# Weight loads of a grouped feed-forward: casting loads on GpSimd's queue replaced by raw int32 loads on SyncE's and casts on VectorE and ScalarE

## What is computed

```python
xn = _layernorm(x, axis=-1)
s = _L0_attn_ref(xn, ...)          # 16 heads, causal
wg = w_gate.astype(f32) / 127      # (3072, 1024) int32, values -127..127
wu = w_up.astype(f32) / 127        # (3072, 1024) int32
wd = w_down.astype(f32) / 127      # (1024, 3072) int32
h  = silu(xn @ wg.T) * (xn @ wu.T)
g  = silu(h @ wd.T)
x  = x + s * g
```

## Time and profile before

| | us |
|---|---|
| median of two timed runs | 3277.18 (3241.79 and 3312.57) |
| profiled execution, whole | 3240.19 |
| its span, slowest core | 3238.7 (cores from 3217.6) |
| PE, DVE, ACT, POOL busy | 2219.3, 880.1, 928.4, 114.0 |

### The profile page before, as it was taken

The page is one execution under the profiler, slowest core; times in us unless marked ns, Lnnn a source line. Parts: engine busy times, 40 slices in busy tenths (PEclk is TensorE's granted clock), DMA queues, the critical chain, the costliest instruction groups (busy, mean ns, idle before and its releaser), DMA issues.

```text
span 3238.7 us, 38701 instructions; the slowest of 8 cores (3217.6 to 3238.7 us)
## 1 busy us (share of the span) xinstructions
PE 2219.3 (69%) x14643; PEld 1170.7 (36%) x14790; DVE 880.1 (27%) x1701; ACT 928.4 (29%) x1245; POOL 114.0 (4%) x216
## 2 busy tenths in 40 slices
PE   2499899984666546786777777065634565877777
PEld 0244444432233213464664665032322221333333
DVE  1544444442232264433222112500200000122122
ACT  2111111102111145463443444132232123222222
POOL 0000011100000000000000000000010000000000
PEclk9699999997878865656556555587856885888888
DMA  4222222202111020202001000533252102011010
GB/s 121 28 30 30 30 33 36 35 3 52 20 17 17 1 52 2 60 2 59 2 2 60 2 2 14 158 56 52 33 81 30 26 0 52 1 52 42 11 52 27
DMA packets 58440, 111.83 MB, mean 35 GB/s; under 512 B 7561, under 2 KB 15755, under 8 KB 55700
## 3 DMA queue, kind: packets, MB, share of 16 engines
q0 software_dynamic: 34112, 52.44, 11.5%
q1 hardware_dynamic: 24148, 56.90, 5.5%
HBM read 142.88 MB, written 18.88 MB: 50 GB/s over the span
## 4 chain that ended last, share of the span: by engine, by line
PE 55%; ACT 17%; DVE 13%; issue 8%; DMA 7%; DVEq 1%; ACTq 0%; SPq 0%; POOL 0%; PEldq 0%; POOLq 0%
PE PS L890 8%; PE PS L724 6%; ACT EB L912 6%; PE PS L1190 6%; PE PS L596 5%; PE PS L605 5%; PE PS L1333 4%; PE PS L1402 4%; PE PS L639 4%; PE PS L1273 2%; DMA PLAND<-Wsel 2%; ACT PRJ L732 2%; DVE PS L895 2%; DVE ACC L650 1%; PE PS L956 1%
## 5 line engine op out<-in xcount | busy, mean ns | idle before, releaser
L890 PE MATMUL PS<-Q,K 64*128 64x128 bf16 x2176 | 274.3, 305 | 125.1 <-ACT EB L912 120.1
L1190 PE MATMUL PS<-XN,W1FULL 128*128 128x512 bf16 x749 | 186.9, 409 | 158.3 <-DMA W1FULL<-Wk 80.1
L912 ACT ACTIVATE EB<-PS,negBh 128x1152 bf16<-128x1152 f32 (+7 forms) x128 | 204.0, 1594 | 258.1 <-DVE PS L895 242.6
L890 PEld LDWEIGHTS PS<-Q,K 64*128 64x128 bf16 x2176 | 211.8, 136 | 154.4 <-issue 143.7
L639 PE MATMUL PS<-HT,WDT 128*128 128x512 bf16 x745 | 191.0, 390 | 38.8 <-DVE HT L622 21.9
L724 PE MATMUL PS<-XN,WBLK 128*128 128x512 bf16 x746 | 207.8, 443 | 12.8 <-DVE K L739 5.1
L895 DVE TENSOR_TENSOR PS<-PS,trinegT 128x128 f32<-128x128 f32 x256 | 76.6, 300 | 439.7 <-PE PS L890 434.6
L596 PE MATMUL PS<-XN,WGT 128*128 128x512 bf16 x752 | 170.6, 382 | 8.5 <-DVE ACC L650 5.6
L1190 PEld LDWEIGHTS PS<-XN,W1FULL 128*128 128x128 bf16 x768 | 78.5, 104 | 263.8 <-issue 189.9
L605 PE MATMUL PS<-XN,WUT 128*128 128x512 bf16 x752 | 168.8, 379 | 0.8
L650 DVE TENSOR_TENSOR ACC<-ACC,PS 128x512 f32<-128x512 f32 x224 | 149.0, 686 | 35.7 <-PE PS L639 34.1
(11 more groups left out here) (162 smaller groups left out, 2579.6 us busy)
## 6 DMA issues: line engine op xcount, KB each, us to landing
PLAND<-Wsel POOLq DMA_DIRECT2D x64, 256.0 KB, 4.2
XF<-xT SPq DMA_DIRECT2D x1, 8192.0 KB, 33.0
XT<-xT SPq DMA_DIRECT2D x4, 2048.0 KB, 10.3
x1park<-XT SPq DMA_DIRECT2D x32, 256.0 KB
X1CH<-x1park SPq DMA_DIRECT2D x8, 1024.0 KB, 8.6
XT<-x1park SPq DMA_DIRECT2D x4, 2048.0 KB, 8.4
outT<-XT SPq DMA_DIRECT2D x32, 256.0 KB
LAND<-wg POOLq DMA_DIRECT2D x16, 256.0 KB, 5.8
```

The lines of the kernel that those rows point to most:

```text
L890: tS = P.op("tensor", lambda t, h=h, gi=gi, tt=tt, off=off: t.matmul(PS[:, off + tt * 128:off + (tt + 1) * 128], head_k(h, ts(tt, 128)), h ...
L912: s.activation(EB2[:, slot, 0:klen], PS[:, 0:klen], AF.Exp, bias=negBh[:, h:h + 1]), inc=True)
L1190: P.op("tensor", lambda t, fc=fc, j=j, n=n: t.matmul(BK(n), W1FULL[:, j, ts(fc, 128)], src_xn[:, j, ts(n, 512)], start=(j == 0), stop=(j = ...
```

## The change

A slice is now loaded by SP as raw int32 into ILAND, a new area of two slots in unused room of the V region. A cast on DVE or ACT, in turn (`cflip`), then writes it as bf16 into the landing buffer, and PE transposes from there as before. All these loads share one new semaphore, dw2. The cast of slice i waits for the whole count of dw2 so far issued, and for PE's reads of its landing buffer. The load of slice i+2 is placed on SP's queue after the cast of slice i, whose slot it reuses. `prep_issue2` issues two loads ahead of a gate/up stage. The first four slices of group 0 are still casting loads of POOL; two raw loads for slices 4 and 5 are issued once the layer norm has read the V region (`tk_var0`).

```diff
-                            lambda li, wsrc=wsrc, hc=hc: P.dma(
-                                "gpsimd", LANDX(li),
+                            lambda il, wsrc=wsrc, hc=hc: P.dma(
+                                "sync", ILAND[:, il, :],
                                 wsrc[hc * 128:(hc + 1) * 128, :],
-                                sem=f"dl{li}")))
+                                sem="dw2")))
...
+    def prep_issue2(g):
         sl = p2_slices(g)
+        P.wait("sync", ilg[0])
+        P.wait("sync", ilg[1])
+        t0 = sl[0][3](0)
+        t1 = sl[1][3](1)
+        return {0: t1, 1: t1}
...
             li = i % 4
-            P.wait("tensor", toks[i])
+            il = i % 2
+            if g == 0 and i < 4:
+                tok_bf = pre_toks[i]
+                tok_cv = None
+            else:
+                ln = D if kind == "gu" else HG * 128
+                eng_c = "vector" if cflip[0] == 0 else "scalar"
+                cflip[0] ^= 1
+                P.wait(eng_c, ("dw2", P.sems["dw2"][1]))
+                P.wait(eng_c, land_guard2[li])
+                if eng_c == "vector":
+                    tok_cv = P.op("vector", lambda v, li=li, il=il, ln=ln:
+                                  v.tensor_copy(LANDX(li)[:, 0:ln],
+                                                ILAND[:, il, 0:ln]), inc=True)
+                else:
+                    tok_cv = P.op("scalar", lambda s, li=li, il=il, ln=ln:
+                                  s.activation(LANDX(li)[:, 0:ln],
+                                               ILAND[:, il, 0:ln], AF.Copy),
+                                  inc=True)
+                ilg[il] = tok_cv
+                tok_bf = tok_cv
+            P.wait("tensor", tok_bf)
...
-            if i + 4 < len(sl):
-                li4 = (i + 4) % 4
-                P.wait("gpsimd", land_guard2[li4])
-                toks.append(sl[i + 4][3](li4))
+            if tok_cv is not None and i + 2 < nsl:
+                P.wait("sync", ilg[(i + 2) % 2])
+                dma_toks[i + 2] = sl[i + 2][3]((i + 2) % 2)
             yield
...
+    P.wait("sync", tk_var0)
+    sl0 = p2_slices(0)
+    _t4 = sl0[4][3](0)
+    _t5 = sl0[5][3](1)
+    dma0 = {4: _t5, 5: _t5}
+    for _ in prep_gen(0, preland, dma0):
         pass
```

More of the change, by code:

```diff
@@ L34 @@
     DMA_SEMS = ("dc", "dx", "dx2", "dst", "dl0", "dl1", "dl2", "dl3",
-                "dr0", "dr1", "dr2", "dr3", "dw")
+                "dr0", "dr1", "dr2", "dr3", "dw", "dw2")
     def __init__(self, nc):
@@ L294, in build @@
     WDT2 = ar.place("WDT2", [128, EC, HG * 128], BF16, oV + (12 << 10))
+    ILAND = ar.place("ILAND", [128, 2, D], I32, oV + (18 << 10))
     HT = ar.place("HT", [128, HG, T], BF16, oW + (18 << 10))
@@ L491, in p2_slices, with prep_gen @@
                 out.append(("gu", w_i, hl,
-                            lambda li, wsrc=wsrc, hc=hc: P.dma(
-                                "gpsimd", LANDX(li),
+                            lambda il, wsrc=wsrc, hc=hc: P.dma(
+                                "sync", ILAND[:, il, :],
                                 wsrc[hc * 128:(hc + 1) * 128, :],
-                                sem=f"dl{li}")))
+                                sem="dw2")))
         for dc in range(EC):
             out.append(("wd", 0, dc,
-                        lambda li, dc=dc, g=g: P.dma(
-                            "gpsimd", LANDX(li)[:, 0:HG * 128],
+                        lambda il, dc=dc, g=g: P.dma(
+                            "sync", ILAND[:, il, 0:HG * 128],
                             wd_d[dc * 128:(dc + 1) * 128,
                                  g * HG * 128:(g + 1) * HG * 128],
-                            sem=f"dl{li}")))
+                            sem="dw2")))
         return out
-    def prep_issue4(g):
-        toks = []
+    ilg = {0: None, 1: None}
+    cflip = [0]
+    def prep_issue2(g):
         sl = p2_slices(g)
[L508 to L514, removed]
+        P.wait("sync", ilg[0])
[3 more added lines that the diff above has]
+        return {0: t1, 1: t1}
+    def prep_gen(g, pre_toks, dma_toks):
         WGTg, WUTg, WDTg = WB[(g + 1) % 2]
@@ L517, in prep_gen @@
         sl = p2_slices(g)
-        toks = list(pre_toks)
         tparity = 0
         first = True
+        nsl = len(sl)
         for i, (kind, w_i, idx, dma_fn) in enumerate(sl):
             li = i % 4
-            P.wait("tensor", toks[i])
+            il = i % 2
[20 more added lines that the diff above has]
+            P.wait("tensor", tok_bf)
             if first:
@@ L570, in prep_gen @@
             prep_done[g] = (lastv, lasts)
-            if i + 4 < len(sl):
-                li4 = (i + 4) % 4
-                P.wait("gpsimd", land_guard2[li4])
-                toks.append(sl[i + 4][3](li4))
+            if tok_cv is not None and i + 2 < nsl:
+                P.wait("sync", ilg[(i + 2) % 2])
+                dma_toks[i + 2] = sl[i + 2][3]((i + 2) % 2)
             yield
     ht_cur[0] = tk_var0
-    for _ in prep_gen(0, preland):
+    P.wait("sync", tk_var0)
[4 more added lines that the diff above has]
+    for _ in prep_gen(0, preland, dma0):
         pass
@@ L586, in build @@
         P.wait("tensor", prev_evac[1])
-        pre4 = prep_issue4(g + 1) if g + 1 < NG else None
+        pre2 = prep_issue2(g + 1) if g + 1 < NG else None
         ht_tok = None
@@ L628, in build @@
         P.wait("tensor", ht_tok)
-        gen = prep_gen(g + 1, pre4) if g + 1 < NG else None
+        gen = prep_gen(g + 1, None, pre2) if g + 1 < NG else None
         evac_toks = [None, None]
```

## The result

The changed kernel took 3453.5 us (median of 11 runs; fastest 3440.2), the kernel before 3242.7 us (10 runs, fastest 3234.1). The ratio, disturbed runs left out, is 1.0635, with a 95% interval from 1.0617 to 1.0652: 6.35% slower, or 206 us on 3242.7. The profiled execution has a span of 3441.1 us, 202 us more than before.

A forecast was written before the change was run, and what follows sets the result against it. The down stage, nearly full on PE and DVE, was taken as the bound. Seven down stages (235 us), first gate matmuls (8) and group 0 (19.5) made 262 us: 3240 + 262 = 3503 us, range 3400 to 3590.

The forecast's parts named there:

- The mechanism: Down stages: the shared count leaves one load in flight, so each period holds release of SP, a load and a cast.
- named in advance: Expected signs: loads never overlapping inside a stage, gate/up and last down stages unchanged, no gain after the feed-forward part.
- The full-clock sum: One down stage that prepares a next group, summed over its casts at full clock: 57.2 us, against 30.6 before.
- The clock: Down stages: half clock expected for two thirds of the stage, giving 64.1 us, between 57.2 at full and 67.6 at half.
- The slow first gate matmuls: After each of seven down stages, the next gate matmuls were to start at half clock: 8 us in all.
- The loads: Raw loads on SP's queue: 3.7 us for a gate/up slice and 2.8 us for a down-weight slice.
- The casts: int32 to bf16 casts, large and small slices: 0.68 and 0.35 us on DVE, 1.04 and 0.49 us on ACT.
- Group 0: Its preparation stands wholly on the path: first gate matmul at 153.5 us instead of 134.04, 19.5 us later.
- The path through PE: Even gate/up slices: transposes, six matmuls, second add, cast; 3.8 us at full clock, hidden under 4.7; 5.3 us at half clock, deciding.
- rival 1: Loads take 2.2 us or two are in flight: down stage 49.0 us, total 3384 us; chance 0.12.
- Rule of the Trainium skill: First byte 0.6 us on SP's queue against 1 us on POOL's; loads 3.5 and 2.5 us, forecast some 15 us lower.
- the head of the stage: Start of a down stage, its first two units and cast 0: 3.0 us at full clock.

The follow-up runs named there:

- Separate counts: Changed kernel with one semaphore per raw slot, so each cast waits for its own load only and two loads are in flight; ratio 1.023 to the kernel before.
- casts ahead: Changed kernel with three raw slots, a semaphore per slot, and each cast placed ahead of the previous slice's transposes; ratio 1.0010 to the kernel before.

## Why the prediction was right, point by point

- **The mechanism: one load in flight, a whole load in each period.** Right. In the seven stages no load started before the one ahead of it had landed, the gate/up stages from group 1 on and the last down stage are as long as before, and nothing is gained behind G, as named in advance. Separate counts took away three fifths of the loss, and with casts ahead as well all of it.
- **The direction and size: 262 us forecast, 206 measured.** Of the 56 us between, some 41 are in the seven down stages, 8 in the first gate matmuls and 5 in group 0. The full-clock sum alone, 57.2 us for a down stage, would have come closer: group 1's took 56.9.
- **The clock.** This is the term that was mis-sized. "I expect half clock for two thirds of the stage" made 64.1 us of 57.2; the windows show 0.91 and 0.80, and an average stage 27.7 us longer than before, not 33.5. Group 2's stage, at 0.80, took 1.7 us more than group 1's at 0.91. I had read the clock off group 0's preparation, where PE did short transposes only; in the down stage six long matmuls stand in each period. Whether that makes the difference was not tried.
- **The slow first gate matmuls, 8 us.** Wrong: in group 1 the gate/up stage took 44.1 us against 44.0. The last six units of a down stage have no cast between them, and the stage ends at full clock.
- **The loads, 3.7 and 2.8 us.** Measured 4.4 us (w_gate), 3.6 us (w_up) and 2.4 us (w_down). A stage waits for one, three and eight of them, so against my sum the large ones are +0.7 - 3 x 0.1 = 0.4 us longer and the small ones 8 x 0.4 = 3.2 us shorter, together 2.8 us less. By this estimate the stage would have been nearer to 54 us than 57 at full clock throughout: that group 1's took 56.9, so near to the full-clock sum, is partly luck, and its share of lower clock made up the difference. The 4.4 us for w_gate is a median of the slowest core; over the eight cores, the exposed w_gate loads had medians from 3.8 to 4.7 us.
- **The casts.** 0.69 and 0.36 us on DVE, 1.06 and 0.52 us on ACT; forecast 0.68, 0.35, 1.04 and 0.49. int32 went at the rate of f32. No table was loaded for the copies.
- **Group 0, 19.5 us.** 14 to 16 us from the landing of x. The small loads were quicker, and the cast of a landed slice ran beside its neighbour's: in the changed kernel casts 12 and 13 both start at 142.78 us.
- **The path through PE.** The prediction had it hidden at full clock and deciding at half clock, with 5.3 us for a period of an even gate/up slice. Both occur: it ended last in 18 of DVE's 42 casts, and in group 1 it took 5.13 us from the end of ACT's cast to the end of DVE's (314.19 to 319.32), at half clock. It set the pace throughout as soon as two loads were in flight, as rival 1 had it: 49.0 us forecast for the stage, 41.9 measured. That sum was too long: with loads landed, ACT's cast of an odd slice (278.19) runs beside the matmuls behind the even slice's transposes, so an odd slice costs about 2.5 us (transposes at 277.01 and 279.51), not 3.5.
- **Rule of the Trainium skill** ("DMA: Bandwidth & Descriptors", section Specifications): a shorter first byte on SP's queue. The runs now have the pair that was missing: same bytes and order, landings on POOL 0.3 us longer for w_down and 0.5 for w_up, and 0.1 shorter for w_gate, which is less than the cores differ by. For w_down and w_up the trace agrees in direction. The release 0.46 us later is a second cost, beside the landing.
- **Where I was surprised**: that the place of the first cast is worth 30 to 40 us. My sum had it in the head of the stage (3.0 us) as if nothing else depended on it. In a serial chain the start counts in full, and it could have started in the gate/up stage, which the loads had already used.

## What to carry to other kernels

Count loads in flight, not buffers: a wait for the total of a shared semaphore makes a cast wait for the load issued after the one it needs, and two slots then behave as one. A load that is hidden by four buffers at 1.8 us a period is fully exposed when its issue hangs on the consumer of the slice before. Where a stage has a serial chain, look for the earliest point at which its first link can run; and place a conversion in the order of an in-order engine one slice ahead of its user.

## What was not expected of the hardware

A load issued from POOL started 0.55 us after the end of the cast that released it, one from SP 0.09 us after; the difference of 0.46 us, met 84 times between the first gate matmul and G, makes 39 of the 50 us between the two kernels there. The longer landings of w_up and w_down would add 27 us (21 x 0.5 + 56 x 0.3), so part of the sum must be covered by other waits. The load of x (8 MB, eight cores at once) took from 29.1 to 37.7 us in profiled executions of kernels that are alike up to there, which is as much as two of the effects measured here; it had to be taken out by comparing stretches. What sets the granted clock between 0.80 and 0.91 in stages of the same instructions was not tried.
